# Gates of the experts: repeated on 128 partitions by sixteen transfers instead of sixteen TensorE products

## The reference, cut to what matters

```python
s = softmax(u @ centroids.T + expert_biases)            # 16 numbers a token
topk_vals, topk_idx = top_k(s, 2)
g_topk = sum(one_hot(topk_idx, 16) * topk_vals[..., None], axis=-2)
xe     = einsum('bsd,eod->bseo', u, Wr) + br            # 16 experts, 128x128 each
routed = einsum('bse,bseo->bso', g_topk, xe)
shared = (einsum('bsd,eod->bso', u, Ws) + sum(bs, axis=0)) / 2
return u + routed + shared
```

## Time and profile before

| | before |
|---|---|
| median of three runs | 1961.29 us |
| profiled execution, own time | 1964.66 us |
| its span, first to last instruction | 1962.9 us |
| PE busy | 1675.1 us, 85% |
| DVE busy | 1529.8 us, 78% |
| ACT busy | 1006.8 us, 51% |
| POOL busy | 915.0 us, 47% |
| DMA queue of SP | 49.54 MB, 8.2% of 16 engines |

### The profile page before, as it was taken

One profiled execution on the slowest core, in us unless ns is written; L12 is line 12 of the kernel. 1 busy time (PEld: TensorE's weight loads), 2 busy tenths in 40 slices (PEclk: granted clock), 3 DMA queues, 4 the chain that ended last, 5 costly groups with the idle time before them and its releaser, 6 DMA issues.

```text
span 1962.9 us, 33706 instructions
## 1 busy us (share of the span) xinstructions
PE 1675.1 (85%) x12063; PEld 1087.1 (55%) x12141; DVE 1529.8 (78%) x3386; ACT 1006.8 (51%) x1998; POOL 915.0 (47%) x1120
## 2 busy tenths in 40 slices
PE   3465889899898989899898989899898989988785
PEld 1234456565655656465655656465665657564544
DVE  4685879798897979798897979789797979783612
ACT  3233464736565564736555464736456463736152
POOL 5453353736364553736454454726355464622102
PEclk9687899999999999999999999989999999999797
DMA  3001010100101010100101010100101010100100
GB/s 98 1 6 54 2 49 8 55 6 28 35 8 54 8 49 7 55 7 19 44 8 54 8 49 7 53 8 8 55 8 54 2 55 2 48 9 24 33 7 6
DMA packets 64617, 53.35 MB, mean 27 GB/s; under 512 B 6018, under 2 KB 63170, under 8 KB 64450
## 3 DMA queue, kind: packets, MB, share of 16 engines
q1 hardware_dynamic: 60898, 49.54, 8.2%
q10 hardware_dynamic: 3552, 1.65, 0.3%
HBM read 8.44 MB, written 4.19 MB: 6 GB/s over the span
## 4 chain that ended last, share of the span: by engine, by line
PE 43%; DVE 36%; issue 6%; ACT 5%; SPq 4%; POOL 3%; DMA 2%; ACTq 1%; DVEq 0%; POOLq 0%
PE bank L902 40%; DVE rmax L725 12%; SPq L308 3%; DVE rmax L722 3%; DVE wkb L672 3%; PE bank L898 3%; DVE prob L805 3%; ACT prob L486 3%; DMA kh<-part 2%; DVE stats L626 2%; DVE kvsum L664 2%; DVE kk L648 1%; DVE tree L635 1%; DVE ksum L659 1%; ACT hat L492 1%
## 5 line engine op out<-in xcount | busy, mean ns | idle before, releaser
L486 ACT ACTIVATE prob<-bank 128x512 f32<-128x512 f32 x640 | 359.4, 600 | 83.2 <-PE bank L902 77.4
L725 DVE TENSOR_REDUCE rmax<-bank 128x1 f32<-128x512 f32 (+2 forms) x768 | 353.5, 504 | 32.9 <-PE bank L902 32.5
L902 PE MATMUL bank<-kh,qh 72*128 72x512 bf16 (+3 forms) x1024 | 262.8, 311 | 54.1 <-DVE rmax L725 39.3
L902 PE MATMUL bank<-qh,kh 75*128 75x512 bf16 (+3 forms) x1024 | 256.8, 305 | 24.2 <-ACT prob L486 20.2
L902 PE MATMUL bank<-wexpT,prob 128*128 128x128 f32 x2048 | 269.4, 279 | 2.2 <-POOL prob L434 1.2
L902 PEld LDWEIGHTS bank<-wexpT,prob 128*128 128x128 f32 x2048 | 256.2, 193 | 20.7 <-issue 15.9
L434 POOL TENSOR_TENSOR prob<-xdT,spread 128x512 f32<-128x512 f32 x128 | 173.7, 1357 | 191.2 <-ACT spread L486 191.1
L486 ACT ACTIVATE spread<-bank 128x512 f32<-128x512 f32 x128 | 76.4, 597 | 295.2 <-PE bank L902 251.0
L902 PEld LDWEIGHTS bank<-qh,kh 75*128 75x128 bf16 x1024 | 99.9, 98 | 203.7 <-ACT prob L486 146.6
L672 DVE RECIPROCAL wkb<-wkb 128x512 f32<-128x512 f32 x64 | 211.6, 3326 | 0.0
L902 PE MATMUL bank<-maskb,identb 128*128 128x128 bf16 x1024 | 196.3, 225 | 0.0
(11 more groups left out here) (210 smaller groups left out, 3415.4 us busy)
## 6 DMA issues: line engine op xcount, KB each, us to landing
qh<-part SPq DMA_DIRECT2D x144, 128.0 KB
kh<-part SPq DMA_DIRECT2D x144, 128.0 KB
x<-in_L_attn_x_dram SPq DMA_DIRECT2D x16, 256.0 KB, 2.9
out_dram<-yo SPq DMA_DIRECT2D x16, 256.0 KB, 2.3
qh<-maxT SPq DMA_DIRECT2D x16, 48.0 KB
wk<-in_L_attn_tm_Wk_dram ACTq DMA_DIRECT2D x1, 256.0 KB
wv<-in_L_attn_tm_Wv_dram ACTq DMA_DIRECT2D x1, 256.0 KB
wr<-in_L_attn_tm_Wr_dram ACTq DMA_DIRECT2D x1, 256.0 KB
```

The costliest lines, as they stand in the source:

```text
L486: raised(act.activation(dst, src, func, **kw), signal)
L725: last = dve.tensor_reduce(rmax[:, j, h:h + 1], S[n % 2][:, col:col + (j + 1) * P], AX_X, ALU.max)
L902: return pe.matmul(out_, w, x, start=start, stop=stop, **kw)
```

## The change

The gates are no longer split. `gT` is the turned `gts` in fp32, 16 partitions x 512 tokens, and `biases` is four fp32 products. For each expert SP issues one transfer that reads row e of `gT` (one partition, 2 KB) 128 times and writes it to 128 partitions of a slot of `prob` (256 KB). DVE (even e) or POOL (odd e) multiplies that slot with `xdT` in place. `gb`, `spread`, `gate_hi`, `gate_rest`, `gate_mid` and `gate_lo` are gone. The slots are now all ten of `prob` (`RING`), and up to eight transfers (`AHEAD`) are issued before the first is used; each of the eight has a semaphore. Six semaphores of the routing became one. Every engine's list is new; in PE's there is one `busy_experts1`, two bf16 products of 512 columns whose result nobody reads, between `cmk0` and `cmk1`.

```diff
+RING, AHEAD = 10, 8
 sp="""
-    4:store 2:heads 0:load 2:max_rows
+    2:heads 3:gate_row0 3:gate_row1 3:gate_row2 3:gate_row6 0:load 3:gate_row7 3:gate_row3 3:gate_row4 3:gate_row8 3:gate_row5 3:gate_row10
+    3:gate_row9 3:gate_row12 3:gate_row11 4:store 3:gate_row15 3:gate_row14 3:gate_row13 2:max_rows
...
-        gT = sb("gT", [P, T], BF16)
-        ug = prob[:, 0:4, :]
-        spread = [sb(f"spread{i}", [P, T]) for i in range(2)]
+        gT = sb("gT", [NE, T])
+        ug = prob
...
+        def gate_row(e):
+            row = gT[e:e + 1, :]
+            return bass.AP(tensor=row.tensor, offset=row.offset, ap=[[row.ap[0][0], 1], [0, P], [1, T]])
...
+            def spread_gate(b, e):
+                until(sp, b, "gT")
+                if e >= AHEAD:
+                    until(sp, b, ("ug", "ug_side")[e % 2], (e - AHEAD) // 2 + 1)
+                if e >= RING:
+                    until(sp, b, "expert_ps", e - RING + 1)
+                sp.dma_start(ug[:, e % RING, :], gate_row(e)).then_inc(sems[f"gate_in{e % AHEAD}"], 16)
...
# POOL, and DVE alike (before: G in place of the spread tile)
             def gated_input(b, e):
-                until(pool, b, "spread_out", e // 2 + 1)
-                if e >= 4:
-                    until(pool, b, "expert_ps", e - 3)
-                raised(pool.tensor_tensor(ug[:, e % 4, :], xdT[:, :], spread[e // 2 % 2][:, :], ALU.mult), "ug_side")
+                until(pool, b, f"gate_in{e % AHEAD}", 16 * (e // AHEAD + 1))
+                raised(pool.tensor_tensor(ug[:, e % RING, :], xdT[:, :], ug[:, e % RING, :], ALU.mult), "ug_side")
...
# PE
             def turn_gates(b):
-                until(pe, b, "gate_hi")
-                until(pe, b, "gate_lo")
-                for j in range(J):
-                    last = mm(G[:, j * P:(j + 1) * P], gate_cols[:, j * PARTS * NE:j * PARTS * NE + P], identb[:, :])
+                until(pe, b, "gates")
+                for j in range(J):
+                    last = pe.transpose(G[0:NE, j * P:(j + 1) * P], gts[:, j, :], ident[:, :])
                 raised(last, "gT_ps")
-            def spread_gate(b, e):
-                until(pe, b, "gT")
-                if e:
-                    until(pe, b, ("ug", "spread_out")[(e - 1) % 2], (e - 1) // 2 + 1)
-                raised(mm(G, owner[:, e:e + 1].broadcast_to([P, P]), gT[:, :]), "gb_ps")
```

More of the change, by code:

```diff
@@ L45 @@
     row_ps=UNITS, rowmax=UNITS, max_part=4, maxT_ps=1, maxT=1, max_in=16, score_ps=UNITS, prob=UNITS, pv=16, pvT=2, back_ps=2, pv_inv=2, att=2,
-    attT_ps=1, attT=1, proj_ps=1, yc=1, xd=1, xdT_ps=1, xdT=1, logit_ps=1, logits=1, lmax=1, lshift=1, lexp=1, lsum=1, linv=1, prob_e=1,
-    pick=9, hot=3, gates=1, gate_hi=1, gate_rest=1, gate_mid=1, gate_lo=1, gT_ps=1, gT=1, gb_ps=16, ug=8, spread_out=8, ug_side=8, expert_ps=16, yd=1, out_ready=1, stored=16,
+    attT_ps=1, attT=1, proj_ps=1, yc=1, xd=1, xdT_ps=1, xdT=1, logit_ps=1, route=6, lexp=1,
+    pick=9, hot=3, gates=1, gT_ps=1, gT=1, **{f"gate_in{e}": 16 * (NE // AHEAD) for e in range(AHEAD)}, ug=8, ug_side=8, expert_ps=16, yd=1, out_ready=1, stored=16,
 )
@@ L61 @@
[L61 to L64, removed]
@@ L73 @@
[L73 to L76, removed]
+        1:mix0 4:u0 3:rowmax13 3:rowmax14 1:mix1 3:rowmax15 1:mix2 4:u2 3:rowmax16 4:u4 3:rowmax17 3:rowmax18 0:moments0 3:rowmax19 3:rowmax20 1:clamp0
@@ L80 @@
[L80 to L87, removed]
@@ new lines @@
+        3:score15 1:v3 3:score16 3:score17 1:r3 3:score18 3:weigh4 3:weigh5 3:score19 3:weigh6 3:score20 2:xcT 3:score21 3:weigh7 3:score22 2:rope0
+        3:score23 3:score24 2:rope1 3:score25 3:score26 2:rope2 3:score27 2:rope3 3:score28 3:weigh8 3:score29 3:score30 3:weigh9 3:weigh10 3:score31
+        3:score32 3:weigh11 3:score33 3:score34 3:score35 3:score36 3:score37 3:back0 3:score38 3:score39 1:read_out0 1:read_out1 1:read_out2 1:read_out3
+        3:weigh12 3:weigh13 3:weigh14 3:weigh15 3:back1 2:attn_v 3:attT 1:xn2T 3:attn_out 1:cmk0 3:busy_experts1 1:cmk1 2:row0 3:xdT 2:row1 2:row2
@@ L260, in build @@
             (ebias[:, :], a["L1_ffn_expert_biases"].rearrange("(o e) -> o e", o=1).broadcast_to([P, NE])),
-            (wexp[:, :, :], a["L1_ffn_Wr"].rearrange("e o d -> o e d")), *((brow[i * NE:(i + 1) * NE], a["L1_ffn_br"]) for i in range(PARTS)),
+            (wexp[:, :, :], a["L1_ffn_Wr"].rearrange("e o d -> o e d")), (brow[:, :], a["L1_ffn_br"]),
             (wsh[:, :, :], a["L1_ffn_Ws"].rearrange("n o d -> o n d")), (bsh, a["L1_ffn_bs"].rearrange("(q n) o -> q n o", q=1)),
@@ L328, in _ @@
             sp.wait_ge(setup["kh_ones"], 4)
-            run("sp", {"load": lambda b: load(b + 1) if b + 1 < B else None, "heads": spread_heads, "max_rows": spread_maxima, "store": store})
+            run("sp", {"load": lambda b: load(b + 1) if b + 1 < B else None, "heads": spread_heads, "max_rows": spread_maxima, **each("gate_row", NE, spread_gate), "store": store})
             until(sp, B - 1, "stored")
@@ L440, in _ @@
                 **each("rope_sum", 2, rope_sum), **each("rest", 2, first_rest), **each("part_lo", 2, third_part),
-                "gate_rest": gate_left, "gate_lo": gate_low, **each("u", SIDE, gated_input),
+                **each("u", SIDE, gated_input),
             }
@@ L585, in _ @@
                 "xdT_out": lambda b: move(b, xdT[:, :], G, "xdT_ps", "xdT"),
-                "route_exp": lambda b: move(b, lex[:, :, :], lsh[:, :, :], "lshift", "lexp", func=ACT.Exp),
-                "gate_hi": lambda b: move(b, gate_part[:, :, 0, :], gts[:, :, :], "gates", "gate_hi"),
-                "gate_mid": lambda b: move(b, gate_part[:, :, 1, :], gate_rest[:, :, :], "gate_rest", "gate_mid"),
-                "gT_out": lambda b: move(b, gT[0:PARTS * NE, :], G[0:PARTS * NE, :], "gT_ps", "gT"),
-                **each("spread", SIDE, lambda b, e: (reached(act, "ug_side", 8 * b + e // 2 - 1), move(b, spread[e // 2 % 2][:, :], G, "gb_ps", "spread_out", e + 1))),
+                "route_exp": lambda b: move(b, lex[:, :, :], lsh[:, :, :], "route", "lexp", 3, func=ACT.Exp),
+                "gT_out": lambda b: (until(act, b - 1, "expert_ps"), move(b, gT[:, :], G[0:NE, :], "gT_ps", "gT")),
             }
@@ L779, in largest @@
                 done = 5 * second
-                until(dve, b, "pick", 5) if second else until(dve, b, "prob_e")
+                until(dve, b, "pick", 5) if second else until(dve, b, "route")
                 raised(dve.tensor_reduce(m[:, :], s[:, :, :], AX_X, ALU.max), "pick")
@@ L801, in gated_input @@
             def gated_input(b, e):
-                until(dve, b, "gb_ps", e + 1)
-                if e >= 4:
-                    until(dve, b, "expert_ps", e - 3)
-                raised(dve.tensor_tensor(ug[:, e % 4, :], xdT[:, :], G, ALU.mult), "ug")
+                until(dve, b, f"gate_in{e % AHEAD}", 16 * (e // AHEAD + 1))
+                raised(dve.tensor_tensor(ug[:, e % RING, :], xdT[:, :], ug[:, e % RING, :], ALU.mult), "ug")
             def add_experts(b):
@@ L962, in busy_maxima @@
             def busy_maxima(b, k):
-                until(pe, b - 1, "ug")
-                until(pe, b - 1, "spread_out")
+                until(pe, b - 1, "gT")
                 keep_busy(G)
@@ L975, in busy_gates @@
             def busy_gates(b, k):
-                until(pe, b, "logits")
+                until(pe, b, "route", 1)
                 keep_busy(G)
@@ L1147, in expert_biases @@
                 for j in range(J):
[L1148 to L1156 removed]
+                    mm(O[:, j * P:(j + 1) * P], gT[:, j * P:(j + 1) * P], brow[:, :], False, False, skip_group_check=True)
             def expert(b, e):
@@ L1173, in _ @@
                 **each("busy_scores", 3, busy_scores), **each("busy_experts", 3, busy_experts), **each("busy_gates", 3, busy_gates),
-                "gT": turn_gates, "shared": start_experts, "biases": expert_biases, **each("gb", NE, spread_gate), **each("expert", NE, expert),
+                "gT": turn_gates, "shared": start_experts, "biases": expert_biases, **each("expert", NE, expert),
             }
```

92 lines of the change are left out of this document (38 added, 54 removed).

## The result

The changed kernel takes 3378.64 us (median of four runs, 3367.84 to 3390.16) against 1961.99: a ratio of 1.723, 95% interval 1.718 to 1.728. The forecast was 3390.

The account below looks back on a forecast made before the run. No single engine bounded the whole; DVE bounded the row stage. A turn: 66.7 + 1.7 + 120 + 1.4 + 3.4 + 5 = 198.2 us, 88.4 more; fifteen give 1326, the last batch 104, so 3390 us, range 1930 to 4320.

Parts of the forecast that it names:

- the slow source partition: Main case: gate rows read from one SBUF partition at about 23.6 GB/s; range 2890 to 4320 us, chance 0.60.
- The bound of the stage: Row stage, 56.55 us and bound by DVE (55.11 busy) before, would lie wholly under 120 us of transfers.
- The transfers: Sixteen gate rows a turn: 1.7 us fixed, plus 120 us, two thirds of 178 us, as rows partly overlap.
- the maxima's late landing: Maxima's transfer, 48 KB to three partitions, landed 3.78 us after issue; read as a 23.6 GB/s limit of few partitions.
- Behind the last row: After the last gate row: POOL's product 1.4 us, experts 13 to 15 3.4, half clock there 3.4 more.
- First part of the ring: Turn from first score to end of gT's copy: 68.0 us, less 1.3 for the gates' splitting, gives 66.7.
- The turn and the end: A turn grows from 109.8 to 198.2 us, fifteen times; the last batch's end from 24.1 to 128.5.
- Costs at nothing: Counted 0: PE's and ACT's freed work, bias products, busy_experts1 (at most 0.5 us) and the moves of other steps.
- Reading one partition as quickly as all: Rival: sixteen transfers take 19 us and hide, gaining 1.4 us a turn: 1940 us; faster or equal, chance 0.20.
- 63 GB/s: Rival: one partition gives the rate of the packets' records, 4.2 us a row; 2180 to 2540 us, chance 0.08.
- DVE and POOL in each other's way: Rival: quick transfers, but DVE's eight products with two SBUF inputs slow by 0.4 us each: 1990 us, chance 0.12.
- A sign that was off: Signs of being right: PE busy under 55%, and rows 0, 1 and 2 landing about 11 us apart.

Follow-up runs that it names:

- the run on one partition: Changed kernel with rows issued in order 0 to 15, all sixteen transfers reading the gates of expert 0 on partition 0: 3921.21 us.
- the last run through DRAM: Also the best version: gates stored in DRAM and read there, engine lists of the kernel before, u0 to u2 and experts 0 to 2 later: 2003.67 us.
- the one that reads 128 partitions: Changed kernel with each of the sixteen transfers reading all 128 partitions of xdT instead of one row of gates: 2019.49 us.
- the run with four groups in turn: Rows issued in order 0 to 15, expert e's gates on partition 4*(e%4) + e//4, against natural order alone (3697.65 us): 2944.33 us.

## Why the prediction was right, step by step

The range, 1930 to 4320 us, held nearly every case that was weighed, so a time inside it says little. What counts is the case that had the most weight, the slow source partition, and its terms.

- *The bound of the stage.* The step "all of the row stage lies under the transfers" held: the first window of the turn has DVE at 38.64 us of 120.
- *The transfers, 1.7 + 120 = 121.7 us.* Measured 122.1. The size is right partly by luck. The rate of one outlet was taken as 23.6 GB/s from the maxima's late landing and is 27, so a row takes 9.7 us and not 11.1; and overlap hides a fifth (122 of 155) where I took a third (120 of 178). The two errors cancel. That there is such an outlet, that it limits reading, and that rows of different groups overlap was forecast and is shown by the runs. That it limits writing too rests on the one late landing alone; no run varied the side that is written.
- *The groups.* The runs show 27 GB/s out of one partition or one group of four, 53 out of two groups, 49 out of partitions 16 apart and 28 out of partitions 32 apart. The Trainium skill's port rule (SBUF — State Buffer, "Door 1: The DMA port swizzle") agrees in each point tested: about 27 GB/s a port, partitions 0 to 3 and those 32 further on the same one, those 16 apart not. The estimate of 154 us for rows one after another, worked out from its figure, is near what the run on one partition shows: 3921 us is 34 us a turn above the changed kernel, and 122 + 34 = 156.
- *Behind the last row, 1.4 + 3.4 and 3.4 for the clock.* Predicted 8.2, measured 6.4: 1.3 for POOL's product (1805.12 to 1806.44) and 5.1 for the three experts. Their 3.4 was counted as 12 products of 279 ns, but the group has 2048 records, eight an expert, and they overlap; 269.4 us for 256 experts are 3.2 for three, so the size was nearly right, by luck. The clock did fall to 0.50, the lower of its two levels (1.2 GHz), while PE waited, and was back at 1.00 by 1810.5, before the last of them was done. So it cost at most 1.9 and not 3.4.
- *First part of the ring.* 66.7 and 1.6 for the clock, 68.3 in all; measured 70.4. Of the 1.3 us for the splitting of the gates, 0.9 came: `gts` ends at 3251.50 and the copy starts at 3252.67 in the last batch, 1.2 us against 2.0 before. The part is longer than forecast, and the trace shows one place where it grows. In PE's new list `row0` stands ahead of `xdT`, and there it waits for the heads' transfer:

```profile
1864.38 0.39 PE L883 MATMUL bank<-kh,qh 72*128 72x512 bf16 x1 [2.12 <-DMA kh<-part]
```

The clock is at 0.50 from 1865 to 1871 (in the kernel before from 1051.8 to 1055, ahead of the routing), and the routing's logits come 56.8 us after the first score (1868.30), against 54.9 before (1056.98). The prediction had set the moves of steps at 0. It is a small matter: from turn to turn this part takes 67.0 to 73.2 us, and 67.7 to 74.3 in the kernel before, the last two turns left out.
- *The turn and the end.* 198.2 against 198.9. Over all 15 the growth is 197.2 - 109.0 = 88.2 us a turn, forecast 88.4. The last batch: 128.5 against 126.7 (3253.26 to 3379.91):

```profile
3252.67 0.59 ACT gT L485
...
3344.36 28.64 DMA prob<-gT
3373.07 1.27 POOL prob L433
3374.39 5.50 PE bank L883 x24
3379.91 0.70 DVE xd L631
```

- *Costs at nothing.* PE's and ACT's freed work: no run shows it by itself; with quick transfers the best version is still 45 us behind, so it doesn't make up for the rest. `busy_experts1`: nothing, as said. The order of the steps: with quick transfers 14 to 60 us; beside slow ones the old lists were not run. The order of the rows, which the prediction didn't weigh, is worth 319 us.
- *The rivals.* Reading one partition as quickly as all: refuted. 63 GB/s, as the packets' records had it: refuted for reading. That such records end before the bytes have arrived is the prediction's reading of the late landing, and stays one. DVE and POOL in each other's way: hardly in the changed kernel, where DVE's product takes 695 ns in the mean, since both engines mostly wait; but in the last run through DRAM and in the one that reads 128 partitions it is there, at 844 and 909 ns. That is 0.17 and 0.23 us a product, where the rival took 0.4 and set the border at 0.17. The quick case was slower than before, as that rival said, at 2019 us in place of its 1990; about half of those 58 us are DVE's longer products.
- *A sign that was off.* PE's busy share was to fall under 55% and is 56%; rows 0 and 2 were to land 22 us apart and do within 18.7 (DVE's products at 1694.85 and 1713.54).

## What to carry to other kernels

The bytes of a transfer and its DMA engines don't tell its cost: count the groups of partitions that it reads, too. Here 256 KB took 9.7 us out of one partition, and landed within 2.6 us out of 128. An SBUF row that is to be repeated on all partitions is better read from DRAM (2050 us here) or from copies that lie in different groups (2173) than from where it lies (3379). The sign in a profile is a DMA share near 0.9 at a tenth of the usual GB/s, or a small transfer that lands later than a large one. Before work moves off an engine, ask whether that engine bounds the stage: here neither PE nor ACT did. DVE does, and its products got longer in the quick versions, because they wait for POOL once both their inputs lie in SBUF.

## What the runs showed of the hardware that was not expected

SP is held by its own issues. The issue of a load or a store takes 0.4 us in the kernel before; behind slow transfers it takes up to 9.6, the time of a row, as these SP rows of the changed kernel show:

```profile
1683.03 17.58 SPq L321 DMA_DIRECT2D prob<-gT  x4
1700.65 9.58 SPq L300 DMA_DIRECT2D x<-in_L_attn_x_dram  x1
1710.29 54.60 SPq L321 DMA_DIRECT2D prob<-gT  x9
```

The first four issues take 17.58 us together, the fifth 9.58: so only about three transfers are in flight at a time (20.9 us from issue to landing, with a row done every 7.6; 32.2 and 10 in the run on one partition), and the eight that the list allows are not reached. This may be why the run with four groups in turn reached only twice one outlet's rate. It was not tested, and does not explain all of it: there too some 2.5 rows were in flight, by 15.9 us from issue to landing and 6.4 a row. What holds the issue back is open.
